# Unit sums in two PSUM banks in turn, and an opening with the branch, the low halves and the weight loads moved

## The chip, the cores and the metric

One core of one Trainium2 chip runs the whole program. The metric is the device time of one execution in microseconds, the median of several.

## The reference

x is 6250 rows of 512 features; src and dst are 100,000 edges, sorted by dst.

```python
deg = max(segment_sum(ones, dst), 1)
xn = layernorm(x)
agg = segment_sum(xn[src], dst)                  # graph part
gnn = xn @ W1.T + b1 + (agg / deg) @ W2.T + b2
qkv = xn @ qkv_w.T ; q, k = relu(q), relu(k)     # 16 heads of 32, linear attention
vk = sum_n v_pad[n] k[n] ; o = (vk q) / (last row of vk q + eps)
x = x + gnn + o @ proj_w.T + proj_b
xn = layernorm(x)
g = top-2 gates of softmax(pooled(xn) @ gate_w + gate_b)   # one pool over all rows
x = x + sum_e g[e] * gelu(gelu(xn @ w1[e] + b1[e]) @ w2[e] + b2[e])   # 2 of 8 experts
```

## The kernel before, in words

The rows are cut into T = 49 tiles of 128. Nearly every f32 operand is split into a high and a low f16 half, and a product is three matmuls (`three`, L857 to L862). The order of the work is written out for each engine, and semaphores join them.

**Opening** (iterations -1 to 16 of the loop over i). Rows of x are normalized in pairs: VectorE takes statistics (`rates`, `moments`), ScalarE writes the normalized row (`rows`, L1306), GpSimd casts the high half (`high_half`, L756), VectorE subtracts the low half (`lows`, L1669), and SyncE stores both halves as a row of `table` in HBM. At i, `pairs_until(i)` says how far the pairs are. In the same iterations TensorE turns a tile (L986), which ScalarE copies (L1370), multiplies k for tile i, and adds to the Gram matrix with tile i-2 (L996 to L998). ScalarE takes relu of k (L1406); GpSimd splits it (L785, L787) up to i = KP = 16, VectorE behind that. Steps on the edges stand in iterations 5 to 11, `judge_lists`, `place_units` and `make_lists` on VectorE at 12, 13 and 14. SyncE loads the next tile of x, eight ahead, and stores the table row in one loop, in order.

**Gathers.** When all table rows are stored, GpSimd reads the register `many`, waits for the last four stores, branches past the slow path (`pool.If(many > 0)`, for lists that are too uneven, not taken here), and issues 782 indirect DMAs (L811). A step n is four of them, 128 rows each, into a ring of four steps. TensorE adds a step into the bank of unit sums with one-hot matmuls (`add_step`, L928); three steps are a unit. A unit's sum is read by ScalarE (`unit_high`, L1342) and then VectorE (`low_half`, L1778), and the first step of the next unit waits for the latter. `add_units` (L946, L947) adds units into the sums of a tile.

**Where the steps stand** is planned when the program is built. `step_plan` walks over the places for steps, ("g", i) and ("k", i) in the k loop from i = FIRST on, ("m", p), and five parts of each layer, with costs in microseconds (K_AT is the time at which the loop reaches FIRST, counted from the first gather), and puts a step where its gathers should have landed. TensorE then takes them in exactly this order.

**Layers** (i = 1 to 48), one tile each: query (TensorE), part 0 of the steps, turn_ah (L1121, turns the tile's means) and turn_p (L1132), part 1, own, part 2, gathered, part 3, mixed, part 4, perhaps add_units, and turn_x2 (L1170), which turns the normalized x2 of the layer before. VectorE's `x2T_low` (L2024) takes the low half of that in the next layer. Steps 188 to 191 stand together in part 3 of layer 48. Behind it come the last tiles, the gate and the experts.

**Weights.** SyncE loads WV and WQ (1 MB each) behind the last table row, G1 and G2 after that. VectorE subtracts the last column from each (`less_last`, L1705).

Of the kernel before, what the change touches and what calls it, by code (L numbers as in the profile page):

```python
# [24 lines left out]
C = D // P  # L25
# [64 lines left out]
FIRST = 19  # L90
TURNED = FIRST + 2
FLOATS, DIFFERENCES, LEAST, FIRSTS, LISTS = (4, 5), 6, 7, 8, 12
EDGE_STEPS = {5: ("dst", 0), 6: ("dst", 1), 7: ("src", 0), 8: ("src", 1), 9: ("first", 0), 10: ("first", 1),
# [6 lines left out]
K_AT, K_STEP, M_PARTS, LAYER, GATHERS, LANDING, ADDING, UNITING = 5.0, 5.75, (7.5, 3.5, 8.0), 11.9, 5.02, 5.0, 0.55, 1.6  # L100
# [137 lines left out]
assert list(TILES_K.values()) == list(range(len(TILES_K))) and SPILLED > KEPT_BEFORE  # L238

# [29 lines left out]
def program(nc, x, src, dst, gw1, gb1, gw2, gb2, qkv_w, proj_w, proj_b, attn_w, attn_b, gate_w, gate_b,  # L269
            w1, b1, w2, b2, out):  # L270
    ctx = ExitStack()
    with ctx:
# [150 lines left out]
        ps_unit = bank[7]  # L423
        ps_o, ps_b, ps_ta, ps_tp, ps_tx = bank[1], bank[2], bank[3], bank[4], bank[0]
# [3 lines left out]
        x2T_bank = lambda t: ps_unit if late(t) else ps_tx  # L428
# [102 lines left out]
        def _(sp):  # L531
# [35 lines left out]
            for t in range(XI, T + XI):  # L567
                r = t - XI
                if t < T:
                    n = TAIL if t == T - 1 else P  # L570
                    sp.wait_ge(s["xn_made"], r + 1)
                    for a, b in parts(n):
                        sp.dma_start(xin[a:b, t % XI, :], x[t * P + a:t * P + b, :]).then_inc(x_loaded[t % XI], 16)
                if r == 4:
                    edge(raw_dst, dst)
                if r == 5:
                    edge(raw_src, src)
                if r == 6:
                    ends_before()
                if r == 14:  # L580
                    with nc.allow_non_contiguous_dma(reason="three biases by output row, 6 KB in all"):
                        for k, b in enumerate((gb1, gb2, proj_b)):
                            sp.dma_start(bcol[:, k], b.rearrange("(a p) -> p a", p=P)).then_inc(s["biases_loaded"], 16)
                n = TAIL if r == T - 1 else P
                sp.wait_ge(s["hi_made"], r + 1)
                sp.wait_ge(s["lo_made"], r + 1)
                stored(sp, r - NS)
                for a, b in parts(n):
                    sp.dma_start(table[r * P + a:r * P + b, :], natural(r)[a:b, :]).then_inc(row_stored[r % NS], 16)
            weight(WV, qkv_w[2 * D:3 * D])  # L590
            weight(WQ, qkv_w[0:D])
# [18 lines left out]

            sp.wait_ge(s["steps_act"], EDGES_ALL)
            weight(G1, gw1)
            weight(G2, gw2)
# [25 lines left out]

            for i in range(FIRST, T + 2):  # L640
                t = i + 2
                if TURNED <= t < T and not by_pe(t):
                    turn(t)
                if i == T - 1:
                    sp.wait_ge(s["k_made"], T)
                    sp.dma_start(raw_w[PJ], proj_w.rearrange("(a p) f -> p a f", p=P)).then_inc(wk_loaded[0], 16)
                if i in TILES_K:
                    spill(TILES_K[i])
# [65 lines left out]
        def _(pool):  # L714
# [62 lines left out]
            for i in range(-1, KP + 1):  # L777
# [21 lines left out]
                if i == FIRSTS:  # L799
                    firsts()  # L800


            pool.wait_ge(s["lists_made"], 1)
            pool.wait_ge(s["steps_act"], ORDER.index(("src", 1)) + 1)
            many = slow_tiles(pool)
            for t in range(T - NS, T):
                stored(pool, t)
# [6 lines left out]
            with pool.If(many > 0):  # L814
                with pool.Fori(0, many) as t:
# [25 lines left out]

            for n in range(STEPS_END):
                u, k = divmod(n, DEEP)
                after(pool, s["step_done"], n - RG + 1)
                for j in lanes_of(n):
                    b = UB * u + DEEP * j + k
                    fetch(slot(n, j), src_col[:, b:b + 1], step_loaded[n % RG])
# [3 lines left out]
        def _(pe):  # L851
# [65 lines left out]
            def add_step(n):  # L917
# [4 lines left out]
                if k == 0:  # L922
                    pe.wait_ge(s["hot_made"], u + 1)
                    after(pe, s["unit_lo"], u)
                for h in range(2):
                    for j in lanes_of(n):
                        a = j * WIDE
                        r = mm(ps_unit[a:a + WIDE, :], hot[:, u % 2, DEEP * j + k, :], ring[:, slot(n, j), h * D:(h + 1) * D],  # L928
# [180 lines left out]
            def turn_ah(t):  # L1109
# [5 lines left out]
                after(pe, s["ahT_lo"], t - 1 if late(t) else t)  # L1115
                if t == 0:
                    pe.wait_ge(s["scales_made"], 4)
# [25 lines left out]
            def gathered(t):  # L1143

                pe.wait_ge(s["ahT_hi" if t in LATE else "ahT_lo"], t + 1)
                if late(t):
                    pe.wait_ge(s["w_made"], T)
                elif t in LATE:
# [14 lines left out]
            def turn_x2(t):  # L1163

                pe.wait_ge(s["xn2_made"], t + 1)
                after(pe, s["x2T_lo"], t - 1 if late(t) else t)
                if late(t):
# [127 lines left out]
        def _(act):  # L1295
# [41 lines left out]
            def unit_high(u):  # L1337
# [4 lines left out]
                F(units[:, u % HOLD, 0:D], ps_unit[:, :], ACT.Copy, scale=SU).then_inc(s["unit_hi"], 1)  # L1342
# [266 lines left out]
        def _(dve):  # L1609
# [113 lines left out]
            def judge_lists():  # L1723
# [9 lines left out]
                link(V.tensor_scalar(slow_i[:], slow[:, 3:4], float(T), None, ALU.mult))  # L1733

# [40 lines left out]
            def low_half(u):  # L1775

                dve.wait_ge(s["unit_hi"], u + 1)
                V.scalar_tensor_tensor(out=units[:, u % HOLD, D:2 * D], in0=ps_unit[:, :], scalar=SU,  # L1778
# [100 lines left out]
            for i in range(-1, T + 2):  # L1879
                for q in pairs_at(i):  # L1880
                    rates(q)
                    moments(q)
                    lows(q)
# [4 lines left out]
                if i == LISTS + 1:  # L1888
                    place_units()
                if i == LISTS + 2:  # L1890
# [455 lines left out]
```

## Time and profile before

| | us |
|---|---|
| median of 3 runs (1461.67 to 1467.06) | 1466.91 |
| the profiled execution | 1465.09 |
| its span | 1462.9 |
| TensorE matmul busy | 1372.7 |
| VectorE busy | 940.4 |
| GpSimd busy | 834.0 |
| ScalarE busy | 610.3 |

Times in the rows count from the start of the span. Busy is the union of the instructions of an engine. [...] Idle time stands in brackets ahead of an instruction, with what ended it; "issue" is idle time that ends with nothing the profile shows.

### The profile page before, as it was taken

The page shows a single profiled execution, that of the slowest core. Times are in us where ns is not written, and L with a number is a line of the kernel's source. Part 1 is how long each engine was busy: PE and PEld are TensorE (multiplying, and loading weights), DVE is VectorE, ACT ScalarE, POOL GpSimd, SP SyncE. Part 2 cuts the span into 40 slices and gives each one's busy share as a digit, 9 for nine tenths or more (in the row PEclk, how much of TensorE's full clock was granted, in tenths as well). Part 3 has the DMA queues.
Part 4 walks back from the last instruction along what each step waited for, and adds up shares of the span by engine and source line. Part 5 has one row for each costly group of instructions (what it writes and reads, how often), then busy time and mean ns, then how long its engine had stood idle before and what let it go on. Part 6 is the DMA issues. An engine that isn't in the chain of part 4 may idle for free.

```text
span 1462.9 us, 22936 instructions
## 1 busy us (share of the span) xinstructions
PE 1372.7 (94%) x7764; PEld 625.1 (43%) x7764; DVE 940.4 (64%) x2087; ACT 610.3 (42%) x938; POOL 834.0 (57%) x907
## 2 busy tenths in 40 slices
PE   7888989999999999999999999899996889999997
PEld 3444434444444444444444444344442344444443
DVE  8877343222566877777777767666764466776677
ACT  5645223232233444444434444333332436555554
POOL 4653777777777777777777777777777200000000
PEclk9999999999999999999999999999998989999998
DMA  6854889998888888888887777877877341223322
GB/s 202 259 184 166 254 224 245 238 253 236 269 276 262 280 273 272 281 270 280 252 247 237 238 250 236 251 239 234 249 239 239 110 145 49 91 90 115 115 86 100
DMA packets 141205, 312.09 MB, mean 213 GB/s; under 512 B 40050, under 2 KB 42636, under 8 KB 141108
## 3 DMA queue, kind: packets, MB, share of 16 engines
q0 software_dynamic: 62560, 205.05, 46.7%
q1 hardware_dynamic: 62608, 77.26, 16.9%
q10 hardware_dynamic: 15940, 28.54, 5.3%
q8 instruction: 56, 0.92, 0.3%
q14 instruction: 41, 0.34, 0.1%
HBM read 260.53 MB, written 45.52 MB: 209 GB/s over the span
## 4 chain that ended last, share of the span: by engine, by line
PE 50%; POOL 25%; issue 10%; DVE 8%; DMA 4%; ACT 2%; SPq 0%; DVEq 0%; ACTq 0%; POOLq 0%
POOL ring L811 24%; PE bank L857 13%; PE bank L858 12%; PE bank L862 12%; PE bank L928 4%; DMA ring<-table,src_col 2%; PE bank L946 1%; PE bank L947 1%; PE bank L1121 1%; PE bank L996 1%; DVE xT L1669 1%; PE bank L997 1%; PE bank L998 1%; DVE st L1659 1%; DVE ring L2290 1%
## 5 line engine op out<-in xcount | busy, mean ns | idle before, releaser
L811 POOL DMA_INDIRECT ring<-table,src_col x782 | 759.6, 971 | 251.1 <-issue 242.7
L857 PE MATMUL bank<-wts,xT 128*128 128x512 f16 x588 | 226.2, 385 | 3.9 <-DVE wts L1875 2.1
L858 PE MATMUL bank<-wts,xT 128*128 128x512 f16 x588 | 226.0, 384 | 0.0
L928 PE MATMUL bank<-ring,hot 128*32 128x512 f16 x1560 | 121.3, 389 | 40.2 <-DMA ring<-table,src_col 32.1
L857 PE MATMUL bank<-wts,work 128*128 128x512 f16 x392 | 152.5, 389 | 1.5 <-ACT work L1463 1.4
L862 PE MATMUL bank<-wts,xT 128*128 128x512 f16 x588 | 152.9, 383 | 0.0
L858 PE MATMUL bank<-wts,work 128*128 128x512 f16 x392 | 151.6, 387 | 0.0
L1351 ACT ACTIVATE work<-bank,rd 128x512 f32<-128x512 f32 x49 | 33.7, 687 | 187.4 <-DVE rd L1832 186.3
L1899 DVE TENSOR_TENSOR work<-work 128x512 f16<-128x512 f32 x32 | 22.3, 696 | 137.6 <-ACT work L1409 137.4
L862 PE MATMUL bank<-wts,work 128*128 128x512 f16 x392 | 101.1, 380 | 0.0
L1593 ACT ACTIVATE work<-work 128x512 f32<-128x512 f32 x98 | 61.8, 630 | 79.9 <-DVE work L2300 78.8
L857 PEld LDWEIGHTS bank<-wts,xT 128*128 128x128 f16 x588 | 57.9, 98 | 76.9 <-issue 21.4
L862 PEld LDWEIGHTS bank<-wts,xT 128*128 128x128 f16 x588 | 58.2, 99 | 71.6 <-issue 4.0
L1778 DVE SCALAR_TENSOR_TENSOR units<-bank,units 128x512 f16<-128x512 f32 x65 | 44.7, 688 | 66.3 <-ACT units L1342 65.6
L1342 ACT ACTIVATE units<-bank 128x512 f16<-128x512 f32 x65 | 38.6, 595 | 116.6 <-PE bank L928 110.6
L858 PEld LDWEIGHTS bank<-wts,xT 128*128 128x128 f16 x588 | 58.1, 99 | 55.2 <-issue 2.2
L2300 DVE SCALAR_TENSOR_TENSOR work<-bank,mix,work 128x512 f32<-128x512 f32 x98 | 69.9, 746 | 15.0 <-PE bank L862 9.8
L2290 DVE SCALAR_TENSOR_TENSOR ring<-work,gexp,ring 128x512 f32 (+1 forms) x98 | 73.3, 748 | 9.2 <-DVE ring L2290 4.1
L857 PE MATMUL bank<-xT,wts 128*128 (+2 forms) x208 | 75.0, 367 | 2.9 <-ACT wts L1571 2.9
L1406 ACT ACTIVATE work<-bank 128x512 f32<-128x512 f32 x49 | 29.1, 594 | 112.3 <-PE bank L862 112.3
L858 PE MATMUL bank<-xT,wts 128*128 (+2 forms) x208 | 75.0, 367 | 0.0
L857 PE MATMUL bank<-wts,ring 128*128 128x512 f16 x196 | 74.3, 379 | 0.0
(307 smaller groups left out, 2523.8 us busy)
## 6 DMA issues: line engine op xcount, KB each, us to landing
x_rows<-work ACTq DMA_DIRECT2D x51, 256.0 KB
ring<-table,src_col POOLq DMA_INDIRECT x782
work<-in_x ACTq DMA_DIRECT2D x48, 256.0 KB
ring<-x_rows SPq DMA_DIRECT2D x12, 1024.0 KB, 5.1
out_x<-ring SPq DMA_DIRECT2D x12, 1024.0 KB
table<-xT SPq DMA_DIRECT2D x45, 256.0 KB, 3.2
ring<-in_x SPq DMA_DIRECT2D x44, 256.0 KB, 3.3
spilled<-work SPq DMA_DIRECT2D x25, 256.0 KB, 3.8
```

Source lines behind the costliest of these rows:

```text
L811: pool.indirect_dma_start(ring[:, k, :], None, table[:, :], bass.IndirectOffsetOnAxis(ap=ap, axis=0)).then_inc(sem, 16)
L857: mm(out_, wh(c), mh(c), start=first and c == 0, stop=False)
L858: mm(out_, wh(c), ml(c), start=False, stop=False)
L862: r = mm(out_, wl(c), mh(c), start=False, stop=last and c == n - 1)
L928: r = mm(ps_unit[a:a + WIDE, :], hot[:, u % 2, DEEP * j + k, :], ring[:, slot(n, j), h * D:(h + 1) * D], start=(k == 0 and h == 0), stop=( ...
L1342: F(units[:, u % HOLD, 0:D], ps_unit[:, :], ACT.Copy, scale=SU).then_inc(s["unit_hi"], 1)
L1351: F(mean_in(t), agg_bank(t)[:, :], ACT.Copy, scale=rd_of(t)).then_inc(s["ah_made"], 1)
L1406: F(k32, k_bank(i)[:, :], ACT.Relu, scale=SK).then_inc(s["k32_made"], 1)
L1593: F(act2[:, j % 2, e], pre[:, j % 2, e], ACT.Gelu).then_inc(s["act_made"], 1)
L1778: V.scalar_tensor_tensor(out=units[:, u % HOLD, D:2 * D], in0=ps_unit[:, :], scalar=SU, in1=units[:, u % HOLD, 0:D], op0=ALU.mult, op1=ALU ...
L2290: r = V.scalar_tensor_tensor(out=y, in0=act2[:, j % 2, e], scalar=gexp[:, e:e + 1], in1=y, op0=ALU.mult, op1=ALU.add)
L2300: V.scalar_tensor_tensor(out=pre[:, j % 2, e], in0=bank[4 + 2 * (j % 2) + e][:, :], scalar=mix[:, 4:5], in1=b2b[:, e], op0=ALU.mult, op1=A ...
```

## The change

Step 0 may stand at i = 18 instead of 19, and K_AT is 7. In the layers, units from TWO_FROM (16 here) on take bank 0 and bank 7 in turn, so a unit's first step waits for the unit two before it. Bank 0 held the turned x2; that now goes to bank 2, where the means are turned, so turn_ah waits for the low half of the x2 turned before, and the last three tiles take other banks. In the opening `lows` runs a pair behind from pair 5 on, with both at the end. `place_units` and `make_lists` go from iterations 13 and 14 to 16, behind the low halves, and judging signals by itself. GpSimd reads `many` in iteration 14, branches ahead of the wait for the last table rows, and waits for the finished lists only at step 3. WV and WQ are loaded at rows 42 and 44 of SyncE's loop, G1 and G2 at iterations 20 and 22.

```diff
-FIRST = 19
+FIRST = 18
...
+BEHIND = 4
...
-K_AT, K_STEP, M_PARTS, LAYER, GATHERS, LANDING, ADDING, UNITING = 5.0, 5.75, (7.5, 3.5, 8.0), 11.9, 5.02, 5.0, 0.55, 1.6
+K_AT, K_STEP, M_PARTS, LAYER, GATHERS, LANDING, ADDING, UNITING = 7.0, 5.75, (7.5, 3.5, 8.0), 11.9, 5.02, 5.0, 0.55, 1.6
+def odd_bank(u):
+    return u >= TWO_FROM and (u - TWO_FROM) % 2 == 0
+def unit_before(u):
+    return max((v for v in range(u) if odd_bank(v) == odd_bank(u)), default=-1)
+def x2_before(t):
+    return sum(e not in LATE for e in SEQ[:max(0, TURN[t] - 1)])
...
+        unit_bank = lambda u: bank[0] if odd_bank(u) else bank[7]
-        x2T_bank = lambda t: ps_unit if late(t) else ps_tx
+        x2T_bank = lambda t: ps_unit if late(t) else ps_tx if t in LATE else ps_q if t == T - 3 else ps_ta
...
+                if r == T - XI + 1:
+                    weight(WV, qkv_w[2 * D:3 * D])
+                if r == T - XI + 3:
+                    weight(WQ, qkv_w[0:D])
...
-            weight(WV, qkv_w[2 * D:3 * D])
-            weight(WQ, qkv_w[0:D])
...
-            sp.wait_ge(s["steps_act"], EDGES_ALL)
-            weight(G1, gw1)
-            weight(G2, gw2)
...
+                if i == FIRST + 2:
+                    sp.wait_ge(s["steps_act"], EDGES_ALL)
+                    weight(G1, gw1)
+                if i == FIRST + 4:
+                    weight(G2, gw2)
...
-            pool.wait_ge(s["lists_made"], 1)
-            pool.wait_ge(s["steps_act"], ORDER.index(("src", 1)) + 1)
-            many = slow_tiles(pool)
-            for t in range(T - NS, T):
-                stored(pool, t)
+                if i == LISTS + 2:
+                    pool.wait_ge(s["lists_made"], 1)
+                    pool.wait_ge(s["steps_act"], ORDER.index(("src", 1)) + 1)
+                    many = slow_tiles(pool)
+            def table_stored():
+                for t in range(T - NS, T):
+                    stored(pool, t)
             with pool.If(many > 0):
+                table_stored()
+                pool.wait_ge(s["lists_made"], 2)
...
+            table_stored()
             for n in range(STEPS_END):
+                if n == RG - 1:
+                    pool.wait_ge(s["lists_made"], 2)
...
-                    after(pe, s["unit_lo"], u)
+                    after(pe, s["unit_lo"], unit_before(u) + 1)
+                    if u == TWO_FROM:
+                        pe.wait_ge(s["matrix_split"], C)
...
+                if not late(t):
+                    after(pe, s["x2T_lo"], T - 3 if t == T - 2 else x2_before(t))
...
+                if t == T - 3:
+                    pe.wait_ge(s["w_made"], T)
+                if t in LATE:
+                    pe.wait_ge(s["unit_lo"], UNITS)
...
                     rates(q)
                     moments(q)
-                    lows(q)
+                    if q < BEHIND:
+                        lows(q)
+                    if q > BEHIND:
+                        lows(q - 1)
+                    if q == PAIRS:
+                        lows(q)
                 if i == LISTS:
                     judge_lists()
-                if i == LISTS + 1:
+                if i == KP:
                     place_units()
-                if i == LISTS + 2:
                     make_lists()
```

## Rows read from the trace of the kernel before

**Rows 1.** The page, the chain that ended last, by engine.
```profile
PE 50%; POOL 25%; issue 10%; DVE 8%; DMA 4%; ACT 2%; SPq 0%; DVEq 0%; ACTq 0%; POOLq 0%
```
**Rows 2.** The gathers' line L811: duration min/median/max in ns, idle us and times.
```profile
L811 POOL DMA_INDIRECT ring<-table,src_col x782: 942/946/2807, 146.8 to 1147.0; - x196
...
  PE bank L928: 8.4, 16
```
**Rows 3.** Timeline of TensorE, 1115 to 1132 us: start, us, line.
```profile
1115.61 0.61 PE L928 MATMUL bank<-ring,hot 128*32 128x512 f16 x8
1120.37 1.04 PE L928 MATMUL bank<-ring,hot 128*32 128x512 f16 x8 [4.14 <-DMA ring<-table,src_col]
1124.73 1.04 PE L928 MATMUL bank<-ring,hot 128*32 128x512 f16 x8 [3.31 <-DMA ring<-table,src_col]
1129.81 1.05 PE L928 MATMUL bank<-ring,hot 128*32 128x512 f16 x8 [4.03 <-DMA ring<-table,src_col]
```
**Rows 4.** Waits, 385 to 1131 us: total us, times, longest.
```profile
PE bank L928 <- DMA ring<-table,src_col: 23.5, 11, 4.1
...
PE bank L928 <- DVE units L1778: 7.8, 8, 1.3
```
**Rows 5.** The chain that ended last, 138 to 147 us: start, us, what.
```profile
138.41 2.02 DMA table<-awb
...
140.54 0.04 POOLq L814
140.59 6.25 issue
```
**Rows 6.** Timeline of GpSimd, 136 to 150 us.
```profile
136.57 0.61 POOL L756 CAST awb<-ring 128x511 f16<-128x511 f32 x1
```
**Rows 7.** Stretches: busy PE, PEld, DVE, ACT, POOL; clock, DMA share, GB/s.
```profile
20.00:138.00 118.00, 104.17 (x571) 51.04 (x570) 96.61 (x212) 68.81 (x110) 67.15 (x87) 0.96 0.61 197
141.00:147.00 6.00, 3.23 (x22) 1.57 (x20) 2.35 (x3) 2.11 (x3) 0.17 (x1) 1.00 1.02 346
```
**Rows 8.** Waits, 20 to 138 us.
```profile
ACT ring L1306 <- DVE nmr L1652: 30.6, 18, 3.9
...
DVE xT L1669 <- POOL xT L756: 13.5, 10, 4.7
...
PE bank L986 <- ACT xT L1370: 4.8, 3, 3.3
```
**Rows 9.** Timeline of TensorE, 84 to 88 and 121 to 124 us.
```profile
84.93 0.91 PE L874 MATMUL bank<-wts,ones 128*128 128x128 f32 x6 [2.76 <-POOL wts L774]
...
122.44 0.62 PE L986 MATMUL bank<-ident,xT 128*128 128x128 f16 x8 [3.28 <-ACT xT L1370]
...
123.11 0.45 PE L858 MATMUL bank<-wts,xT 128*128 128x512 f16 x1
123.35 0.63 PE L857 MATMUL bank<-wts,xT 128*128 128x512 f16 x1
123.78 0.63 PE L858 MATMUL bank<-wts,xT 128*128 128x512 f16 x1
```
**Rows 10.** Timelines of VectorE and GpSimd at 157 us.
```profile
156.75 2.28 DVE L1705 TENSOR_TENSOR wts<-wts 128x2044 f32<-128x2044 f32 x1
...
157.18 2.67 POOL L811 DMA_INDIRECT ring<-table,src_col  x1 [0.30 <-issue]
```
**Rows 11.** Timeline of two layers, around 579 and 624 us.
```profile
578.78 0.68 DVE L2024 TENSOR_TENSOR xT<-bank,xT 128x512 f16<-128x512 f32 x1
578.88 0.60 PE L1121 MATMUL bank<-ident,work 128*128 128x128 f32 x4
...
623.06 0.68 DVE L2024 TENSOR_TENSOR xT<-bank,xT 128x512 f16<-128x512 f32 x1
...
624.15 0.66 PE L1121 MATMUL bank<-ident,work 128*128 128x128 f32 x4
```
**Rows 12.** Timeline of TensorE, 156 us.
```profile
156.18 0.61 PE L928 MATMUL bank<-ring,hot 128*32 128x512 f16 x8 [0.50 <-DMA ring<-table,src_col]
```

More of the change, by code:

```diff
@@ L238 @@
 assert list(TILES_K.values()) == list(range(len(TILES_K))) and SPILLED > KEPT_BEFORE
+STARTS = {n // DEEP: at for at in PLAN for n in PLAN[at] if n % DEEP == 0}
+TWO_FROM = min(u for u in range(UNITS) if isinstance(STARTS[u][0], int))
+def odd_bank(u):
[4 more added lines that the diff above has]
+    return sum(e not in LATE for e in SEQ[:max(0, TURN[t] - 1)])
 def ends(i, *at):
@@ L927, in add_step @@
                         a = j * WIDE
-                        r = mm(ps_unit[a:a + WIDE, :], hot[:, u % 2, DEEP * j + k, :], ring[:, slot(n, j), h * D:(h + 1) * D],
+                        r = mm(unit_bank(u)[a:a + WIDE, :], hot[:, u % 2, DEEP * j + k, :], ring[:, slot(n, j), h * D:(h + 1) * D],
                                start=(k == 0 and h == 0), stop=(h == 1 and k == DEEP - 1 or last), skip_group_check=True,
@@ L1147, in gathered @@
                     pe.wait_ge(s["w_made"], T)
+                    pe.wait_ge(s["x2T_lo"], T - 2)
                 elif t in LATE:
@@ L1341, in unit_high @@
                     act.wait_ge(s["agg_made"], last_tile(u - HOLD) + 1)
-                F(units[:, u % HOLD, 0:D], ps_unit[:, :], ACT.Copy, scale=SU).then_inc(s["unit_hi"], 1)
+                F(units[:, u % HOLD, 0:D], unit_bank(u)[:, :], ACT.Copy, scale=SU).then_inc(s["unit_hi"], 1)
             def keep_ah(t):
@@ L1733, in judge_lists @@
                 link(V.tensor_scalar(slow_i[:], slow[:, 3:4], float(T), None, ALU.mult))
+                dve.sem_inc(s["lists_made"], 1)
             def place_units():
@@ L1777, in low_half @@
                 dve.wait_ge(s["unit_hi"], u + 1)
-                V.scalar_tensor_tensor(out=units[:, u % HOLD, D:2 * D], in0=ps_unit[:, :], scalar=SU,
+                V.scalar_tensor_tensor(out=units[:, u % HOLD, D:2 * D], in0=unit_bank(u)[:, :], scalar=SU,
                                        in1=units[:, u % HOLD, 0:D], op0=ALU.mult, op1=ALU.subtract).then_inc(s["unit_lo"], 1)
```

## The prediction

> **What bounds the kernel now.** I read the page first. The chain of work that ended last is half TensorE and a quarter the gathers of GpSimd [rows 1], so two chains run nearly level, and the reader has to find which one ends last, and where. The gathers' own line answers the first half [rows 2]: 782 of them, median 946 ns each, the first at 146.8 us and the last at 1147.0, and GpSimd sat idle for TensorE only 8.4 us in 16 places; the rest of its idle time is the 0.3 us between two gathers. So from its first gather on, GpSimd runs at its own pace of some 5.1 us a step of four, whatever the others do. TensorE's timeline answers the second half [rows 3]: near the end of the layers it has finished step 188 at 1116.2 us and then stands idle 4.14, 3.31 and 4.03 us before steps 189, 190 and 191, each time until a gather has landed. That is 11.5 us that TensorE has in hand there. Step 191 starts 1129.8 us into the span, 983 us after the first gather, and the last 333 us hang on it. The gather chain sets the end: its start, plus 983 us, plus 333 us. A microsecond taken from TensorE in the layers is worth nothing, one taken from the first gather's start is worth one microsecond, as long as TensorE keeps up.
>
> How much TensorE could keep up with: over the layers it waited 23.5 us in 11 places for gathers (the 11.5 us among them) and 7.8 us in 8 places for VectorE's low half of a unit [rows 4].
>
> What holds the first gather: the last table row lands at 140.4 us, GpSimd branches at once, and then 6.25 us pass with nothing that the profile shows before the first gather at 146.84 [rows 5]. GpSimd's last cast of the opening began at 136.57 [rows 6]. Before that lies the opening, where TensorE is busy 104.2 of 118 us and VectorE 96.6 [rows 7]. The waits there form a ring: ScalarE waits for VectorE's mean and rate (30.6 us, 18 times), VectorE for GpSimd's high half before its low half (13.5 us, 10 times), TensorE for ScalarE's copy of a turned tile (4.8 us, 3 times) [rows 8].
>
> **The branch.** The slow-list branch is moved ahead of the wait for the last table rows. It costs 6.25 us alone [rows 5]. In the new order GpSimd reaches it when its last cast is issued, 136.6 to 137.2 us [rows 6], so on the old clock the first gather could go at about 143, or, if the branch is nearly free, at 140.4 plus the 0.3 us that a gather takes to issue, 140.7. During those 6.25 us the 16 DMA engines were busy throughout (share 1.02 [rows 7]) with the weight loads, which the change moves away, so the branch may well be shorter. The nearest row is its own, though: I take a first gather at 142.8, a gain of 4.0 us; bounds 3.3 (137.2 + 6.3 = 143.5) and 6.1. The register read moves into the GpSimd loop, beside its idle time there.
>
> [...]
>
> **The low halves a pair behind.** VectorE then no longer waits for GpSimd and sends the next mean and rate sooner. What that is worth is TensorE's share, because k(16) on TensorE releases the last GpSimd work: TensorE was idle 3.28 us before 122.44, with ScalarE's copy behind VectorE's list judging, and its matmuls then start 0.43 us apart instead of 0.22 [rows 9]; nine of them do so, 1.9 us more. I take 4 of these 5.2 us, since the judging stays on VectorE. The 2.76 us before 84.93 (and the same 1.9 us of slow matmuls behind it) end with a GpSimd pass that stood behind high halves held by the same ring: 1.5 of 4.7 us. Placing units and making lists leave iterations 13 and 14, behind which TensorE's timeline shows no wait: nothing. The price is on SyncE: the next load of x stands behind the store of a row whose low half now comes a pair later. Eight tiles of buffer still leave more than one pair period for the landing, so I cost it at nothing; where two pairs come in one iteration it may cost 2 us in all, an estimate. Sum 5.5 us; bounds -2 (x late, nothing gained) and 11.8 (both waits with their slow stretches, 9.9, and 1.9 of smaller ones).
>
> **The moved weights.** WV and WQ are issued 7 and 5 rows before the end, G1 and G2 at loop iterations 20 and 22 behind SyncE's transposed tiles. Each is needed two or more iterations later, so none is waited for, and the opening's DMA share of 0.61 [rows 7] has room for 2 MB more. But the subtraction on WV then runs earlier on VectorE, behind the placed units and the lists, right where the gathers now start. How a gather fares beside it: the same line on WQ takes 2.28 us from 156.75, and the gather that starts at 157.18 takes 2.67 instead of 0.95 [rows 10]. Loss 0 (it may miss the gathers, or have held the first one before as well) to 1.7 us; I take 1.0. [...]
>
> **Two banks for unit sums.** Step 3u of the layers no longer waits for unit u-1's low half: 7.8 us off TensorE [rows 4]. In exchange x2's turned rows move to the bank of the turned means, and turn_ah now waits for the low half of the x2 turned before. Where a gather step stands between query and turn_ah, that low half ends 0.4 us before the turn (623.06 + 0.68 against 624.15 [rows 11]); most layers look like it. Where none stands there it ends 0.6 us after the turn's start (578.78 + 0.68 against 578.88), so a wait of 0.6 to 1.0 us; I take 0.85. The planner's rules with FIRST 18 and K_AT 7 leave 13 of 48 layers without a step in that place, against 6: 13 times 0.85 is 11 us more on TensorE. Net 3 us slower there, off the path.
>
> **FIRST 18.** Step 0 stands one iteration earlier, 6.3 us by the planner's costs (K_STEP and an added step). Before, TensorE stood 0.5 us for it, 9.3 us after the first gather [rows 12]; now it waits about 6 us, once, and is then so much further back against the gathers. TensorE's hand at step 188: 11.5 + 12 (its other waits for gathers in the layers) - 6 - 3 = 14 us. It stays off the path.
>
> **Sum.** First gather earlier by 4.0 + 5.5 - 1.0 = 8.5 us; the 983 and 333 us stand. The profiled execution took 1465.1 us (span 1462.9), 1.8 under the median of 1466.9. 1466.9 - 8.5 = 1458.4 us.
>
> **Rivals.** A, the opening keeps its pace: the ring's waits are held by something else (the judging, GpSimd's passes on edges), and only the branch is hidden: 4.0 - 1.0 = 3 us, 1464. For it: VectorE waits for GpSimd only 10 times in 49 rows, and TensorE is busy 88% already. B, TensorE becomes the bound through turn_ah: VectorE's passes come later than in the rows, and most of 45 layers wait instead of 13. From 14 us in hand it decides when such waits exceed 11 + 14 = 25 us over the layers; with 45 times 0.85 = 38 us the end is 13 us later than forecast, 1471, and at 1.1 us a layer 1483. Against it: 0.4 us of margin in the usual layer. C, the branch costs next to nothing with idle DMA engines and the opening gives most of its 9.9 us: 6.1 + 9 = 15, 1452.
>
> **How the numbers follow.** A measurement tells this kernel from no change at 0.5%, 7.3 us. The forecast holds 0.55, A 0.25, C 0.12, B 0.08. The forecast's own width (gain 6 to 11) puts 0.40 of it beyond 7.3 us and 0.15 within; with C faster is 0.52, with A same is 0.41, and B gives slower 0.07. Bounds: gain 3.3 - 2 - 1.7 = -0.4 to 6.1 + 11.8 = 17.9; without the outer tenth on either side 1451 to 1467.
>
> **What would show it.** First gather near 138 instead of 146.8, and the last near 1138; GpSimd's gap after the branch beginning before the last row lands; GpSimd's last cast near 131 instead of 136.6; one more gather of 2.7 us near 139; no wait of a matmul of L928 for a unit's low half in the layers, but some 13 waits of turn_ah for x2's low half; TensorE still idle for gathers before steps 189 to 191. The prediction is wrong if TensorE does not wait there (B), or if the distance from first gather to step 191 is not 983 us.

## The result, and the profile after

The changed kernel takes 1452.07 us (median of 4 runs, 1447.39 to 1455.07), beside 1466.99 for the kernel before (4 runs, 1461.67 to 1469.58). The ratio is 0.9905, 95% interval [0.9887, 0.9924]: 13.9 us faster (11.1 to 16.6), where 8.5 was forecast. The profiled execution is the slowest of the four, 1455.07 (span 1453.2), 3.0 over their median, while the profile of the kernel before is 1.9 under its own. So the two profiles lie only 9.7 us apart, and some 4 us of the gain are in no profile.

The page, the chain that ended last, by engine, and then the gathers' line (it answers to [rows 1, 2]):
```profile
PE 66%; POOL 9%; DVE 7%; issue 4%; DMA 4%; ACT 1%; SPq 0%; ACTq 0%; DVEq 0%; POOLq 0%
```
```profile
L837 POOL DMA_INDIRECT ring<-table,src_col x782: 942/949/2547, 134.0 to 1136.1; - x196
...
  issue: 228.9, 751
  PE bank L961: 13.5, 30
```
The first gather starts at 134.00 us instead of 146.84, 12.8 earlier. GpSimd was held by TensorE for 13.5 us in 30 places instead of 8.4 in 16, and the chain that ended last runs more through TensorE: the two chains are closer than before.

TensorE's timeline at the end of the layers (it answers to [rows 3]), and its waits from 385 to 1131 us (it answers to [rows 4]):
```profile
1108.79 1.05 PE L961 MATMUL bank<-ring,hot 128*32 128x512 f16 x16
1113.62 1.04 PE L961 MATMUL bank<-ring,hot 128*32 128x512 f16 x8 [3.78 <-DMA ring<-table,src_col]
1117.97 1.04 PE L961 MATMUL bank<-ring,hot 128*32 128x512 f16 x8 [3.31 <-DMA ring<-table,src_col]
```
```profile
PE bank L1156 <- DVE xT L2069: 10.9, 15, 4.5
PE bank L961 <- DMA ring<-table,src_col: 7.7, 3, 3.8
PE bank L961 <- DVE wts L2031: 3.7, 1, 3.7
PE bank L905 <- DVEq L1999: 1.6, 1, 1.6
PE bank L1210 <- DVE work L2100: 0.9, 1, 0.9
PE bank L888 <- DVE work L2063: 0.8, 1, 0.8
```
Steps 188 and 189 now run in one piece (x16). TensorE still waits for gathers before 190 and 191, 7.1 us in all, so the gather chain still sets the end, with less to spare. Step 191, the last of these lines, starts 984.0 us after the first gather (before 983.0), and 335.2 us follow it (before 333.1). The account closes: 12.8 - 1.0 - 2.1 = 9.7 us of span. The waits for a unit's low half are gone from the steps (7.8 us before), and turn_ah (L1156) waits for x2's low half instead, 10.9 us in 15 places. The 3.7 us were in no term of the prediction: the first unit that takes bank 0 waits for `matrix_split`, the split of the matrix that stood in that bank. It comes with the plan and not with the bank alone: two banks with the old constants show no such wait, and with one bank under the new plan TensorE stands 3.93 us at that place (before 393.77) for a unit's low half.

The chain from the last stores to the first gather (it answers to [rows 5]):
```profile
123.39 6.53 DMA table<-xT
...
130.36 2.69 DMA table<-awb
...
133.12 0.88 issue
134.00 2.21 POOL ring L837
136.21 0.30 issue
136.51 0.95 POOL ring L837
```
Where 6.25 us of nothing stood behind the last table row, 0.88 stand now. The first gather itself is long, 2.21 us. VectorE's timeline shows what runs beside it, the subtraction on WV (it answers to [rows 10]):
```profile
132.89 2.28 DVE L1745 TENSOR_TENSOR work<-work 128x2044 f32<-128x2044 f32 x1
```
The opening (the columns are those of [rows 7]) and the waits in it (they answer to [rows 8]):
```profile
20.00:138.00 118.00, 109.73 (x607) 55.07 (x605) 97.05 (x218) 72.63 (x116) 78.69 (x90) 0.96 0.70 221
```
```profile
ACT ring L1346 <- DVE nmr L1692: 12.9, 15, 2.1
...
PE bank L905 <- POOL wts L798: 3.6, 1, 3.6
```
ScalarE waits 12.9 us for VectorE's mean and rate instead of 30.6, and of VectorE's waits for a high half in x's tiles (13.5 us in 10 places) 0.3 us in one place is left. GpSimd's last cast ends at 128.5 us instead of 137.2, 8.7 earlier. In this execution 1.3 us are given back behind it: the last row landed 3.3 us after the cast, now 4.5.

### The profile page after: what moved, and what is told of

Read it like the earlier page. It is cut to its first block, busy times and chain, and to the rows that moved or that the text cites. A ratio compares the mean times of both kernels' runs of the same rounds, so it can differ in the third digit from the quotient of the medians.

```text
span 1453.2 us, 22935 instructions
## 1 busy us (share of the span) xinstructions
PE 1372.8 (94%) x7756; PEld 625.6 (43%) x7756; DVE 938.2 (65%) x2087; ACT 609.1 (42%) x937; POOL 843.0 (58%) x907
## 4 chain that ended last, share of the span: by engine, by line
PE 66%; POOL 9%; DVE 7%; issue 4%; DMA 4%; ACT 1%; SPq 0%; ACTq 0%; DVEq 0%; POOLq 0%
PE bank L888 16%; PE bank L893 15%; PE bank L889 15%; POOL ring L837 9%; PE bank L961 6%; PE bank L979 2%; PE bank L980 2%; PE bank L1029 2%; PE bank L1156 2%; PE bank L1030 2%; PE bank L1031 2%; DMA ring<-table,src_col 2%; DMA work<-in_x 1%; PE bank L1167 1%; DVE work L2063 1%
## 5 line engine op out<-in xcount | busy, mean ns | idle before, releaser
L961 PE MATMUL bank<-ring,hot 128*32 128x512 f16 x1560 | 122.6, 393 | 26.7 <-DMA ring<-table,src_col 22.7
```

Of the source, the lines that this page charges most:

```text
L961: r = mm(unit_bank(u)[a:a + WIDE, :], hot[:, u % 2, DEEP * j + k, :], ring[:, slot(n, j), h * D:(h + 1) * D], start=(k == 0 and h == 0), s ...
```

## The experiments

The gain of each run below is its ratio's distance from 1, times 1465 us. The intervals are some 2 us wide on either side, so a difference of 2 or 3 us between two rows is not resolved. First gather and step 191 (counted from the first gather) come from one profiled execution each. "Old plan" is FIRST 19 and K_AT 5, the planner's constants of the kernel before.

| kernel | ratio [95%] | gain | first gather | to step 191 |
|---|---|---|---|---|
| changed | 0.9905 [0.9887, 0.9924] | 13.9 | 134.0 | 984.0 |
| before + branch part | 0.9963 [0.9949, 0.9978] | 5.4 | 141.1 | 985.3 |
| before + two banks | 1.0002 [0.9987, 1.0016] | -0.3 | 144.3 | 979.8 |
| changed, low halves back | 0.9936 [0.9920, 0.9951] | 9.4 | 140.2 | 981.6 |
| changed, branch back | 0.9904 [0.9887, 0.9921] | 14.1 | 132.3 | 981.4 |
| changed, weights back | 0.9945 [0.9930, 0.9961] | 8.1 | 133.8 | 987.5 |
| changed, one bank | 1.0035 [1.0024, 1.0047] | -5.1 | 129.7 | 1000.5 |
| changed, one bank, old plan | 0.9890 [0.9864, 0.9916] | 16.1 | 134.4 | 982.5 |
| changed, old plan | 0.9914 [0.9891, 0.9936] | 12.6 | 134.2 | 981.5 |
| one bank, old plan, firsts later | 0.9878 [0.9859, 0.9896] | 17.9 | 126.8 | 985.3 |
| one bank, old plan, weights ten rows earlier | 0.9905 [0.9885, 0.9926] | 13.9 | 133.4 | 986.5 |
| one bank, old plan, both of these | 0.9892 [0.9874, 0.9911] | 15.8 | 127.8 | 982.3 |
| one bank, old plan, lists back | 0.9913 [0.9894, 0.9932] | 12.7 | 134.7 | 980.2 |

### How far one profile can be trusted

The kernel with one bank (under the new plan) and the kernel with the branch back have the changed kernel's opening, apart from the branch at its end, and yet in their profiles GpSimd's last cast ends at 125.3 us in both, 3.3 earlier than the changed kernel's 128.5. TensorE's timeline shows where they part, first the changed kernel, then the one with one bank:
```profile
80.61 1.62 PE L905 MATMUL bank<-wts,ones 128*128 128x128 f32 x6 [3.56 <-POOL wts L798]
82.01 0.63 PE L1029 MATMUL bank<-work,xT 128*128 128x512 f16 x1
82.44 0.63 PE L1030 MATMUL bank<-work,xT 128*128 128x512 f16 x1
```
```profile
80.03 0.91 PE L905 MATMUL bank<-wts,ones 128*128 128x128 f32 x6 [3.55 <-POOL wts L798]
80.77 0.38 PE L1027 MATMUL bank<-work,xT 128*128 128x512 f16 x1
80.98 0.38 PE L1028 MATMUL bank<-work,xT 128*128 128x512 f16 x1
```
The stretch from 80 to 90 us of each (the columns are those of [rows 7]):
```profile
80.00:90.00 10.00, 9.39 (x41) 5.12 (x42) 7.01 (x16) 2.96 (x5) 4.21 (x5) 0.69 0.74 247
```
```profile
80.00:90.00 10.00, 9.97 (x63) 5.82 (x64) 7.83 (x21) 4.96 (x8) 6.29 (x8) 1.00 0.72 240
```
The wait of 3.5 us is the same. From 80 to 86 us the granted clock was 0.50 in the one and 1.00 in the other, and the matmuls start 0.43 us apart in the one and 0.22 in the other. Of the 3.3 us, 0.6 were there before this wait. Five profiles with this opening (in two of them the loads stand elsewhere) have a clock of 0.66 to 0.69 in that stretch and a last cast that ends between 128.5 and 130.0; two have 1.00 and 125.3. So one first gather of this opening is good to some 5 us only, and a difference below that between two profiles is not the edit's until the clock of this stretch has been compared. The openings with the kernel before's order spread by 2.0 us (135.1 to 137.2).

### The opening, part by part

**The branch alone, on the kernel before.**
```diff
+                if i == LISTS + 2:
+                    ...
+                    many = slow_tiles(pool)
-            for t in range(T - NS, T):
-                stored(pool, t)
             with pool.If(many > 0):
+                table_stored()
...
+            table_stored()
```


> The kernel before with the early branch alone (register read in the loop, branch ahead of the wait for the last rows, finished lists awaited at step 3). Theory: the 6.25 us gap goes to about 1 us, the first gather is at 141.5 us, and the end 4 to 5 us earlier: 1460 to 1462. If the undone branch of the other run is the measure, 2 us; if VectorE's pass on WV holds the first gathers instead, 3 us. Rival (TensorE takes it back): no change.

The chain that ended last, there:
```profile
138.15 2.04 DMA table<-awb
...
140.26 0.88 issue
141.14 1.16 POOL ring L813
```
The branch hides wholly: the first gather comes 5.7 us earlier and the time is 5.4 us less, near the bound of 6.1 that the prediction gave. Its term of 4.0 was too small. It let the branch take its 6.25 us from the end of the last cast, here 136.9; the last row landed at 140.2 and the branch did not delay the gather, so it took 3.3 us at the most. Note that the weight loads still stand behind the last row here, and that the gain comes in full.

**The branch back behind the stores, all else changed.**
```diff
+            table_stored()
             with pool.If(many > 0):
-                table_stored()
```


> The changed kernel with the wait for the last table rows ahead of the branch again (the register is still read early). Theory: the whole branch shows again between the landing of the last row and the first gather. It took 6.25 us in the kernel before, with the weight loads beside it; here 3 to 6.3 us, so the first gather 2 to 5.4 us later and the time 2 to 5.4 us longer, about 1456. [...] Rival (the branch cost nothing by itself; the gap before was VectorE's pass on WV that ended at 146.65): gap about 1 us, no loss.

The chain there, and then the stretch of the gap (the columns are those of [rows 7]):
```profile
129.11 0.04 POOLq L514
...
129.24 3.02 issue
132.26 1.16 POOL ring L837
```
```profile
129.20:132.20 3.00, 3.00 (x22) 1.59 (x21) 2.75 (x3) 1.02 (x1) 0.00 (x0) 1.00 0.25 33
```
The branch takes 3.0 us with the DMA engines at a share of 0.25, where it took 6.3 at 1.02 [rows 5, 7], and 5.8 in the kernel with only two banks added, where the share was 0.96. The share is not the only difference: in the 3.0 us run the register is read earlier too, and no run parts the two. VectorE's pass on WV, the rival of the expectation, does not end the gap: with two banks alone the first gather starts at 144.31, 0.3 us before that pass ends. The first gather at 132.3 is earlier than the changed kernel's 134.0 since this is one of the two openings at full clock. What the jump ahead still saves is 2.1 us of gap, and the times do not resolve it (0.9904 beside 0.9905, and a median of 1449.26 where about 1456 was expected). So the branch's gain and the weights' overlap: 5.4 us alone, nothing measurable on top of the moved loads.

**The low halves back in place.**
```diff
-                    if q < BEHIND:
-                        lows(q)
-                    if q > BEHIND:
-                        lows(q - 1)
-                    if q == PAIRS:
-                        lows(q)
+                    lows(q)
```


> The changed kernel with one part undone: lows(q) in its old place for every pair. Theory (gather chain: time = first gather + 984 us to step 191 + 335 us): the opening's ring of waits comes back, the last cast moves from 127.9 us toward 134 us, the first gather from 134 to about 140, and the time is 5 to 7 us over the changed kernel, about 1458. Rival (placing the units and making the lists at iteration 16, not the low halves, made the opening shorter): the last cast stays within 2 us of 128 and the time within 2 us of the changed kernel, about 1453. If TensorE in the layers set the end, a later first gather would not show in the time at all.

The chain there:
```profile
136.19 0.70 DVE awb L1709
...
137.32 1.97 DMA table<-awb
...
139.35 0.88 issue
140.24 1.33 POOL ring L837
```
The last cast is 7.6 us later, the first gather 6.2, and the time 4.5 us more by the ratios (5 to 7 expected), whose intervals just overlap (0.9936 [0.9920, 0.9951] beside 0.9905 [0.9887, 0.9924]). The rival, that placing and lists made the opening shorter, asked for a last cast within 2 us of 128 and is out. Of the last cast's 8.7 us the low halves bring 7.6 in these two profiles, and 6 to 11 by the spread of the changed opening.

**WV, WQ, G1 and G2 back behind the last row.**
```diff
-                if r == T - XI + 1:
-                    weight(WV, qkv_w[2 * D:3 * D])
-                if r == T - XI + 3:
-                    weight(WQ, qkv_w[0:D])
...
+            weight(WV, qkv_w[2 * D:3 * D])
+            weight(WQ, qkv_w[0:D])
...
+            sp.wait_ge(s["steps_act"], EDGES_ALL)
+            weight(G1, gw1)
+            weight(G2, gw2)
```


> The changed kernel with the four weight loads in their old places on SyncE (WV and WQ behind the last table row, G1 and G2 behind them). Theory: the last rows of the table land up to 1 us sooner, VectorE's pass on WV comes later and beside the gathers, TensorE waits some 3 us for WV's rows off the path; first gather at 133 to 135, time within 2 us of the changed kernel. Rival (4 MB of loads beside the first gathers delays them, and the move of the loads carries part of the gain): first steps land 3 us or more later and the time is 3 to 5 us longer, about 1456.

TensorE's timeline and then GpSimd's, there:
```profile
161.37 1.04 PE L958 MATMUL bank<-ring,hot 128*32 128x512 f16 x8 [11.08 <-DMA ring<-table,src_col]
```
```profile
171.15 0.95 POOL L834 DMA_INDIRECT ring<-table,src_col  x1 [3.75 <-PE bank L958]
```
The first gather is as early as ever, 133.8, but 4 MB of loads run beside the gathers behind it (DMA share 1.06 in the 25 us after it, 0.73 in the changed kernel). The second step's rows land so late that TensorE stands 11.08 us before 161.37; then TensorE is behind and holds the ring, and GpSimd waits 2.33 us at 162.70 and 3.75 at 171.15. The kernel loses 5.8 us, as the rival of the expectation had it, and 3.5 of them show as a longer way to step 191. Why the step lands so late is open. The volume of the loads does not explain it alone: from 152 to 158 us, with TensorE still waiting, the DMA share was 0.22 and 45 GB/s moved. And with the branch alone on the kernel before the same loads stood in the same place, the share in the 25 us from 141 was 1.04, and TensorE waited 2.5 us at the most for a gather. At least two things differ there: step 0 stands an iteration later, and SyncE issues its first transposing DMA (`turn`) at 158.8 us, some 16 us behind G1 and G2, which took 13.4 to land; here it is issued at 139.4, 3 us behind them, and they took 18.7. The weights back under the old plan were not run. The prediction saw in the moved weights only their price.

**Placing and lists back to iterations 13 and 14** (on the kernel with one bank and the old plan, below).
```diff
-                if i == KP:
+                if i == LISTS + 1:
                     place_units()
+                if i == LISTS + 2:
                     make_lists()
```


> From the changed kernel with one bank and the planner's old two constants (1447.4 us), the placing of the units and the making of the lists go back to iterations 13 and 14 of the opening, where the kernel before has them. The prediction held this part for worth nothing. By it: first gather within 1 us and time within 1.5 us of 1447.4. Rival (GpSimd's list making stands ahead of first halves that TensorE waits for): a new TensorE wait of 2 to 4 us in the opening, the last cast later by as much, and 1450 to 1452.

The last cast ends at 130.6 us instead of 128.7, with less of the slow clock (0.83 against 0.68 from 80 to 90 us), the first gather starts 0.4 later, and no new wait of TensorE shows (7.8 us of waits from 20 to 138 us against 7.6). The ratio is 0.9913 against 0.9890, with intervals that overlap; the median of 1451.41 is outside what the theory allowed and inside the rival's range, whose wait did not come. So the prediction's "nothing" is neither shown nor refuted, and a loss of 3 us is not excluded.

### The layers

**Two banks alone, on the kernel before.**
```diff
-                    after(pe, s["unit_lo"], u)
+                    after(pe, s["unit_lo"], unit_before(u) + 1)
...
+                if not late(t):
+                    after(pe, s["x2T_lo"], T - 3 if t == T - 2 else x2_before(t))
```


> The kernel before with the two banks and the moved x2 turns alone. Theory: gathers start at 147 us as before and set the end; the 8 us of waits for a unit's low half go, some waits of turn_ah for x2's low half and one of 3 us at the first unit in the layers (it waits for the split mixing matrix) come; time within 2 us of before, 1463 to 1467. Rival (two banks speed the kernel by themselves): 1458 or less.

TensorE's waits there, 385 to 1131 us:
```profile
PE bank L950 <- DMA ring<-table,src_col: 21.2, 12, 4.7
PE bank L1145 <- DVE xT L2053: 6.0, 6, 2.2
```
Waits for units turned into waits of turn_ah, six of them, as many as the planner's rule counts (four in the layers that it names), and the ratio is 1.0002: off the path, as predicted. The wait of 3 us at the first unit in the layers that was expected did not come.

**One bank, all else changed.** The edit takes back the two waits above, `unit_bank` and `x2T_bank`.


> The changed kernel with one bank for unit sums and x2's turned rows in their own bank, as before. Theory: TensorE's waits for the low half of a unit come back (about 8 us over the layers) and those of turn_ah for x2's low half go (about 11 us); both lie off the path, TensorE still waits for gathers before steps 190 and 191, and the time is the changed kernel's within 2 us, 1450 to 1454. Rival (two banks carry part of the gain): 4 to 8 us longer, 1456 to 1460, and no wait for gathers before step 191.

TensorE's waits there, 385 to 1131 us, then the timeline of one place, all engines, and what GpSimd's shows behind it:
```profile
PE bank L959 <- DVE units L1810: 28.8, 17, 4.7
PE bank L959 <- DMA ring<-table,src_col: 9.3, 3, 4.1
```
```profile
851.62 0.60 ACT L1373 ACTIVATE units<-bank 128x512 f16<-128x512 f32 x1
...
854.58 0.69 DVE L1962 SCALAR_TENSOR_TENSOR work<-bank,ksb 128x512 f32<-128x512 f32 x1
...
857.13 0.68 DVE L1810 SCALAR_TENSOR_TENSOR units<-bank,units 128x512 f16<-128x512 f32 x1
...
857.96 1.04 PE L959 MATMUL bank<-ring,hot 128*32 128x512 f16 x8 [4.65 <-DVE units L1810]
```
```profile
867.74 0.94 POOL L837 DMA_INDIRECT ring<-table,src_col  x1 [3.75 <-PE bank L959]
```
The theory fell: it allowed 2 us, and the loss is 19 (1.0035 against 0.9905), more than the rival's 4 to 8. ScalarE has read the unit by 852.2, but VectorE's queue takes the low half only after the passes of normal, score and weigh, 5 us later, and TensorE stands for it. In the new plan the 8 layers from 29 to 36 end a unit in part 1 and begin the next in part 2 or 3; in the old plan four do (1 to 4, none with part 2; the expectation below says three). These waits put TensorE behind, GpSimd waits for free slots of the ring (31.0 us over the run, 13.5 in the changed kernel), and step 191 moves from 984.0 to 1000.5 us after the first gather. The gathers still end the chain (TensorE waits 3.52 and 4.10 us for them before steps 190 and 191), but their own pace is now TensorE's doing. The first gather is 4.3 us earlier than the changed kernel's, by the clock shown above and not by the edit, so these two profiles are 9.4 us apart where the ratios say 19.

**One bank and the planner's old constants (FIRST 19, K_AT 5); and the old constants with two banks.**
```diff
-FIRST = 18
+FIRST = 19
...
-K_AT, K_STEP, M_PARTS, LAYER, GATHERS, LANDING, ADDING, UNITING = 7.0, 5.75, (7.5, 3.5, 8.0), 11.9, 5.02, 5.0, 0.55, 1.6
+K_AT, K_STEP, M_PARTS, LAYER, GATHERS, LANDING, ADDING, UNITING = 5.0, 5.75, (7.5, 3.5, 8.0), 11.9, 5.02, 5.0, 0.55, 1.6
```


> The changed kernel with one bank for unit sums and with FIRST 19 and K_AT 5: what is left of the change is the opening, the branch and the weight loads. Theory (two banks pay only under the new plan, in which eight layers end a unit in part 1 and begin the next in part 2 or 3, where VectorE takes the low half late; the old plan has three such layers, none with part 2): TensorE's waits for a unit's low half fall from 25 us to about 8 us, the gathers are hardly held up, and the time is 1452 to 1457. Rival (two banks pay for themselves in any plan, since TensorE is the bound as soon as the gathers start 13 us earlier): 1462 or more, with gathers held up by TensorE.

> The changed kernel with FIRST 19 and K_AT 5 alone undone, both banks kept. Theory (the gather chain sets the end here, TensorE has several us in hand): time within 2 us of the changed kernel, about 1451, fewer waits at step 0, first gather and distance to step 191 the same. Rival (the new places of the steps carry part of the gain): 3 us or more longer.

TensorE's waits, 385 to 1131 us, of the first kernel:
```profile
PE bank L959 <- DMA ring<-table,src_col: 23.1, 11, 4.1
PE bank L959 <- DVE units L1810: 7.4, 7, 1.3
```
With the old plan one bank costs nothing that can be measured: 0.9890 (the median of 1447.39 is better than the 1452 to 1457 expected), and TensorE has its old hand at the end again (4.08, 3.10 and 3.87 us before steps 189 to 191, 11.1 in all). Two banks under the old plan give 0.9914, as expected. The two layer edits of the change therefore belong together: the plan needs the second bank, and the pair of them brings nothing that can be measured (0.9905 against 0.9890). What can be measured of the gain is the opening's, with the branch and the loads.

### A next version

From the kernel with one bank and the old plan, three more. The first moves the steps that issue GpSimd's `firsts` one iteration later:
```diff
-FLOATS, DIFFERENCES, LEAST, FIRSTS, LISTS = (4, 5), 6, 7, 8, 12
+FLOATS, DIFFERENCES, LEAST, FIRSTS, LISTS = (4, 5), 6, 7, 8, 13
...
-EDGE_STEPS = {5: ("dst", 0), 6: ("dst", 1), 7: ("src", 0), 8: ("src", 1), 9: ("first", 0), 10: ("first", 1),
-              11: ("first", 2)}
+EDGE_STEPS = {5: ("dst", 0), 6: ("dst", 1), 7: ("src", 0), 8: ("src", 1), 10: ("first", 0), 11: ("first", 1),
+              12: ("first", 2)}
```


> From the changed kernel with one bank and the planner's old two constants (1447.4 us), the three iterations of the opening that also issue the first layers' GpSimd lists come one row pair later (10, 11, 12; the lists at 13). In the profile of the changed kernel TensorE waits 3.56 us at 80.61 us for GpSimd's first halves, and this should take that wait and a part of the slow-clocked stretch behind it away. Theory (the first gather sets the end, and TensorE the opening): the first gather comes 3 to 5 us earlier and the time is 1443 to 1445. Rival (the last row of the table waits for its stores and the loads beside them): the last cast comes earlier, the last row less than 1 us, and the time stays within 1 us of 1447.4.

The second loads WV and WQ at `r == T - XI - 9` and `r == T - XI - 7` instead of + 1 and + 3, which is ten rows of the table, not the ten row pairs of its expectation. The third has both edits.


> From the same kernel, the loads of WV and WQ are issued ten row pairs earlier, so that the last stores and the last table row meet no bulk load. In the changed kernel the last row lands 4.5 us behind the last cast, in the kernel before 3.3 us. Theory: it lands 3.3 us behind the cast, the first gather is 1.2 to 1.5 us earlier, and the time is 1 to 1.5 us less (about 1446). Rival: the loads, now beside TensorE's busiest stretch of the opening, hold up its x loads, TensorE waits there 2 us or more, and the time is 1447 to 1450.

> Both edits of the two other kernels together (the iterations 10 to 12 with the lists at 13, and the weight loads ten row pairs earlier). Theory: their gains add, since both only move the first gather: 4 to 6 us earlier, a time of 1441 to 1444. Rival: one eats the other (the loads fall beside the moved iterations), and the time is that of the better one alone.

TensorE's timeline of the first of these, at the place shown above (the wait of 3.56 us before 80.61):
```profile
82.40 0.83 PE L905 MATMUL bank<-wts,ones 128*128 128x128 f32 x6
83.07 0.38 PE L1027 MATMUL bank<-work,xT 128*128 128x512 f16 x1
83.28 0.38 PE L1028 MATMUL bank<-work,xT 128*128 128x512 f16 x1
```
The wait for GpSimd is gone, and so are the matmuls 0.43 us apart behind it. The last cast ends at 122.6 us and the first gather starts at 126.8, in the third kernel 123.7 and 127.8. By the first gather that is 7 us; by the times it is 0.9878 against 0.9890, 1.8 us and inside both intervals. Part of the 7 us is the clock and not the wait: beside the two openings that waited and kept the full clock (125.3) the last cast is 2.6 us earlier. So the profile shows the step as expected and the time less than the 1443 to 1445 expected.

In the second kernel the last row does land 3.2 us behind the last cast instead of 4.5, but so it does without the edit in two of the others (3.3 with the old plan and two banks, 3.2 with the lists back), and no gain shows: 0.9905, 1452.12 us where 1446 was expected. The third was to add up both gains and give 1441 to 1444; it took 1448.33 us (0.9892), so they do not add. The first is the lowest ratio of all, 1446.89 us. It beats the kernel before clearly; beside the changed one its interval (0.9878 [0.9859, 0.9896] and 0.9905 [0.9887, 0.9924]) overlaps.

## Why the prediction was right, point by point

**What bounds it: right, and the size too small.** The first gather moved 12.8 us, the two distances behind it moved by 1.0 and 2.1 us, and the time by 13.9. Holding TensorE up (one bank under the new plan) is what breaks the 983 us, as the prediction named for its failure. But the forecast of 8.5 us lies outside the measured 11.1 to 16.6, and 1452.07 stands only 1 us inside the stated range: two terms were too small, the branch and the opening.

**The branch: right mechanism, mis-sized.** 4.0 forecast, 5.4 alone. The gap before the first gather is 0.88 us, not the 0.3 allowed; the branch took at most 3.3 us where it hides and 3.0 where it was seen with the loads moved, not the 6.25 that the term carried over from its own row. It took 6.3 and 5.8 us with the DMA engines at a share of 1.02 and 0.96, and 3.0 with them at 0.25; what GpSimd waits for in it no run shows.

**The low halves: right mechanism, mis-sized.** 5.5 forecast for the opening; the last cast gained 8.7 and the last row's landing gave back 1.3, in profiles that are good to some 5 us. The prediction counted two waits of TensorE; the 3.28 us one, then before 122.44, shrank to 0.74 (now before 116.59). The clock from 120 to 130 us rose from 0.83 to 1.00. The other, 2.76 us before 84.93, did not shrink: it is 3.56 before 80.61, so the 1.5 us taken for it were not there. All TensorE's waits from 20 to 138 us fell from 13.8 to 7.9 us, and the smaller ones made 4.2 of that, which the prediction put into its bound only, as 1.9. That is the mis-sized term. That x arrives late did not happen.

**The moved weights: the step that failed.** It was costed at a loss of 1.0 with nothing on the other side. The loss was the full bound: 2.21 and 1.46 us for two gathers of 0.95, 1.8 us in all, the first beside the subtraction on WV and the second beside a pass that builds one-hot rows (137.86). But left in their place, in this kernel, the loads would have cost 5.8 us. It would be easy to say that the 6.25 us of the branch had covered them before, and that the change took this cover away; but the branch part alone, on the kernel before, took it away too, and its gain came in full. So the price belongs to the loads together with the other edits, and which of these it is stays open. The row of the kernel before, 2.67 us instead of 0.95 beside the same line [rows 10], gives the full 1.7 us; the 1.0 was less only because the pass might have missed the gathers, and it did not. What holds a gather beside it no run shows.

**Two banks and FIRST 18: right as a whole, wrong in a reason.** turn_ah waits 10.9 us in 15 places (11 in 13 forecast). That the sum fits is partly luck: 4.5 of it is one wait, before 1055.52, where VectorE had stood 4.5 us for a load of x, and the other fourteen come to 6.4, 0.46 each and not 0.85. The first steps wait 5.77, 3.56 and 4.16 us (6 forecast, once), and TensorE's hand is 7.1 us, not 14: the wait for `matrix_split` (3.7) and smaller ones in the layers (the last three of the list above come to 3.3, before 1.1) would make up most of the difference, by the sum alone. "A microsecond taken from TensorE in the layers is worth nothing" held in the kernel before and with the old plan, and held no more in the new plan: with one bank its 28.8 us of unit waits in 17 places cost 19. The prediction carried the 7.8 us of unit waits over from the old plan into the new one; there, with one bank, they are over three times as long.

**Rivals.** C (1452, given 0.12) hit the median, though its mechanism is only half right, so that is luck in part: the branch hides wholly, but not because it is free, and the opening gives 8.7 less 1.3. A and B did not occur; B's mechanism, TensorE behind through waits on VectorE, did occur with one bank.

**Still open.** Why 7 us of first gather in the next version bring 2 in the time. In the profiles the distance from the first gather to step 191 was 985.3 there against 982.5, and the end behind it 333.4 against 332.6; that is 3.6 of them. The rest is that one bank with the old plan was profiled at 1451.67, in an execution with the slow clock (0.68 from 80 to 90 us), while its median is 1447.39. Its five times spread over 8.8 us (1444.33 to 1453.13), as one would expect if this clock differs from execution to execution, and those of the two kernels without the wait over 2.6 and 3.4 us. That the clock makes this spread is not shown, since only one execution of each kernel was profiled. Open too is which edit makes the weights in their old place cost 5.8 us.

## What to carry to other kernels

A part of a change that looks like a price only should be undone by itself as well: here the moved loads carry 5.8 us of the gain. Whether they do so depends on what else has moved: with the branch part alone they stood in their old place and no loss showed. Where an order is planned when the program is built, waits read from the old order are no measure for the new one: list which pairs of work become neighbours in the new plan, and read their distance on the engine between them, in its own queue order. Two edits that each look free or harmful alone (a plan, a bank) should be tried as the four combinations, since only that shows that the pair brings nothing that can be measured. And before a first gather, or any other time that comes from one profile of each kernel, is compared, compare the granted clock of the stretches ahead of it.

## What the runs showed of the hardware that was not expected

A branch on GpSimd's queue, with the issue of the gather behind it, took 6.3 us with the DMA engines at a share of 1.02, 5.8 at 0.96 and 3.0 at 0.25. A gather beside a VectorE subtraction of 2.28 us on two operands took 2.21 instead of 0.95, and 3.21 in the one-bank kernel, where it started 0.1 us behind it. After one and the same wait of 3.5 us TensorE got a clock of 0.50 for 6 us in one execution and 1.00 throughout in another (80 to 90 us), and the openings' last casts lie 3.3 us apart, 2.7 of it behind this wait. And the gathers' pace itself varies: from the first gather to step 191 it took 979.8 to 986.5 us in the twelve kernels (of fourteen) other than the changed one with one bank and the one with the weights back, with mean gathers of 965 ns in the first and 974 in the last, so a gain of 2 us ahead of it is not to be seen in one profile.
